# Scores of a windowed attention in 64x64 tiles of the array, with loads and the last steps in another order

## The reference

```python
q, k, v = heads of x @ Wq.T, x @ Wk.T, x @ Wv.T      # 16 heads of 16 features
q, k = l2norm(q), l2norm(k)
rel = pos[None, :] - pos[:, None]                    # key minus query
mask = (rel < 0) | (rel >= 128)                      # a key lies 0 to 127 ahead
attn = softmax(q @ k.T - abs(rel) * slope_of_head, masked)
x = layernorm(x + (attn @ v) @ Wo.T)
w1b, w2b = alpha1 * sign(w1), alpha2 * sign(w2)      # alpha: mean of |w| in a row
x = layernorm(x + gelu(x @ w1b.T + b1) @ w2b.T + b2) # 1024 hidden
```

## Time and profile before

| what | value |
|---|---|
| time, median of 3 runs | 373.69 us (373.42 to 374.68) |
| the profiled execution's own time | 373.84 us |
| its span, first to last instruction | 372.1 us |
| mean granted TensorE clock | 0.992 |
| busy: PE, PEld, DVE, ACT, POOL | 358.0, 243.9, 318.2, 310.0, 274.5 us |
| DMA moved | 38.31 MB |

### The profile page before, as it was taken

The page is one execution under the profiler, slowest core; times in us unless marked ns, Lnnn a source line. Parts: engine busy times, 40 slices in busy tenths (PEclk is TensorE's granted clock), DMA queues, the critical chain, the costliest instruction groups (busy, mean ns, idle before and its releaser), DMA issues.

```text
span 372.1 us, 11965 instructions
## 1 busy us (share of the span) xinstructions
PE 358.0 (96%) x3933; PEld 243.9 (66%) x3933; DVE 318.2 (86%) x856; ACT 310.0 (83%) x539; POOL 274.5 (74%) x418
## 2 busy tenths in 40 slices
PE   8699999999999999999999999999999999999991
PEld 5445567766766776676676667775666666666671
DVE  3967789998898988888998997869789999999995
ACT  3579789888898898898899999887888888887873
POOL 1169999899999999999999999857554754754321
PEclk9989999999999999999999999999999999999998
DMA  6757944564464446467676754303303404404113
GB/s 225 147 80 173 193 93 117 105 121 87 111 124 101 111 100 127 100 156 162 132 140 143 160 106 82 58 3 60 58 0 58 114 18 98 114 17 97 58 57 113
DMA packets 99490, 38.31 MB, mean 103 GB/s; under 512 B 84736, under 2 KB 98432, under 8 KB 99328
## 3 DMA queue, kind: packets, MB, share of 16 engines
q1 hardware_dynamic: 99456, 37.89, 46.7%
HBM read 12.72 MB, written 4.19 MB: 45 GB/s over the span
## 4 chain that ended last, share of the span: by engine, by line
PE 62%; DVE 24%; issue 5%; DMA 4%; SPq 2%; ACT 1%; DVEq 1%; POOL 0%; POOLq 0%
PE ps L392 14%; PE ps L402 13%; PE ps L435 9%; PE ps L372 8%; PE ps L411 6%; DVE prob L1150 4%; DVE w L1150 4%; PE ps L532 4%; PE ps L419 3%; DVE zstats L1170 3%; DVE resid L1198 3%; PE ps L566 2%; PE ps L426 2%; DVE z L1160 2%; SPq L273 2%
## 5 line engine op out<-in xcount | busy, mean ns | idle before, releaser
L1363 POOL TENSOR_SCALAR_AFFINE_SELECT prob<-prob 128x512 f32<-128x512 f32 x252 | 154.4, 648 | 14.0 <-ACT prob L673 13.4
L673 ACT ACTIVATE prob<-ps 128x1024 f32<-128x1024 f32 (+1 forms) x128 | 122.2, 1009 | 11.6 <-PE ps L372 11.5
L402 PE MATMUL ps<-wqkv,xt 128*128 128x512 f32 x124 | 60.4, 610 | 1.4 <-DVE qkn L934 1.1
L532 PE MATMUL ps<-yT,sgn 128*128 128x512 f16 x256 | 61.1, 379 | 0.0
L745 ACT ACTIVATE ps<-ps,bias,alpha 128x512 f32<-128x512 f32 x64 | 47.9, 750 | 15.6 <-PE ps L532 12.5
L1431 POOL TENSOR_TENSOR resid<-z,resid 128x256 f32 (+1 forms) x31 | 22.6, 728 | 46.0 <-DVE z L1160 46.0
L392 PE MATMUL ps<-prob,vdiag 128*17 128x128 f32 x1024 | 51.4, 274 | 0.0
L392 PE MATMUL ps<-prob,vnext 128*17 128x128 f32 x992 | 50.0, 273 | 0.0
L372 PE MATMUL ps<-qkT 64*128 64x256 f16 (+1 forms) x512 | 38.8, 270 | 2.1 <-DMA qkT<-parts 2.1
L532 PEld LDWEIGHTS ps<-yT,sgn 128*128 128x128 f16 x256 | 25.0, 98 | 22.6
L435 PE MATMUL ps<-wo,oT 128*128 128x256 f32 x128 | 36.2, 405 | 0.0
(11 more groups left out here) (115 smaller groups left out, 679.8 us busy)
## 6 DMA issues: line engine op xcount, KB each, us to landing
xt<-in_xT SPq DMA_DIRECT2D x32, 128.0 KB, 2.1
resid<-in_x SPq DMA_DIRECT2D x32, 128.0 KB, 2.2
out_dram<-resid SPq DMA_DIRECT2D x7, 512.0 KB, 2.9
w<-in_w2T SPq DMA_DIRECT2D x1, 1024.0 KB, 8.1
w<-in_w1T SPq DMA_DIRECT2D x4, 256.0 KB, 3.3
w_nat<-in_w SPq DMA_DIRECT2D x4, 256.0 KB, 3.6
wqkv<-in_wqkvT SPq DMA_DIRECT2D x3, 256.0 KB, 4.1
qkT<-parts SPq DMA_TRANSPOSE x32, 4.3
```

The source lines that it names most:

```text
L402: mm = nc.tensor.matmul(ps[:, QK[slot % 2], :], xt[:, slot, k, :], wqkv[:, k, 0:2 * D], start=(k == 0), stop=(k == DC - 1))
L532: mm = nc.tensor.matmul(ps[:, bank, :], sgn1[:, c, P * k:P * k + P], yT[:, par, a, c, :, :], start=(m == 0), stop=(m == 2 * DC - 1))
L673: nc.scalar.activation(to, scored, ACT.Exp, scale=QK_SCALE ** -2).then_inc(exp_done, 1)
L1363: return nc.gpsimd.affine_select(out=at, in_=at, compare_op=ALU.is_ge, fill=0.0, base=-near, pattern=[[0, CH], [1 if near else -1, P]], ch ...
```

## The change

- **Scores.** Each chunk's four matmuls (64 rows of two heads by 128 keys, 256 queries each) become eight: 64 rows by 64 keys, so four tiles of the array, and 192 queries each. The first 64 keys meet the past queries and the first half of the own ones, the last 64 the second half of the past ones and the own ones. The quarter of the window that is left out is masked anyway; the exponential still reads it, so the four banks are cleared once at the start. The order of the products stays: t, then hp, then the key halves.
- **qkT.** Queries must now lie side by side, past then own, so `qkT` is laid out with the slot inside, and has a fifth slot for the queries of slot 0 again. From block 4 on, SP issues a second transpose, of the queries alone, right behind that of slot 0 (7 more in all, half a block each). PE (chunk 0) and ACT (`high_halves`) wait for it at slot 0, on a new semaphore `again_in`.
- **PE waits.** Each chunk also waits for `consts`.
- **Probabilities.** `OWN_AT` and `NEAR_AT` put the near halves at 0 and 1, the own ones at 2 to 5.
- **Loads.** The residual rows of blocks 0 and 1 are issued ahead of block 4's transpose, those of 2 and 3 behind it, with a semaphore each; DVE waits for the first pair in `add_output(0)`, for the second after its step 4.
- **Start.** The first `keep_warm` writes bank 2, the second comes after two waits; DVE clears four more banks.
- **Drain.** `hidden_low(0, 0, 0)` goes ahead of `round_of(NB - 2)`, `row_stats(NB - 4)` behind `hidden_low(0, 1, 0)`.

```diff
-QSLOT = (0, 2, 1, 3)
-OWN_AT, NEAR_AT = (0, 4, 1, 5), (2, 3)
+OWN_AT, NEAR_AT = (2, 3, 4, 5), (0, 1)
...
-        qkT = sb("qkT", [P, XS, 2 * (H // 2), P], F16)
+        qkT = sb("qkT", [P, 2 * (H // 2), XS + 1, P], F16)
...
-                sp.dma_start_transpose(qkT[:, QSLOT[s]],
+                sp.dma_start_transpose(qkT[:, :, s, :],
                                        parts[:, s % 2].rearrange("p h a d -> p (h a d)")).then_inc(qk_in[s % 2], 16)
+                if s == 0 and not (isinstance(n, int) and n == 0):
+                    sp.dma_start_transpose(qkT[:, 0:H // 2, XS, :],
+                                           parts[:, 0, 0:H].rearrange("p h a d -> p (h a d)")).then_inc(again_in, 16)
...
             load_block(XS + 3, 3)
+            for n in range(2):
+                sp.dma_start(resid[:, n, :], x[n]).then_inc(first_resid[0], 16)
             turn_parts(XS, 0)
-            for n in range(XS):
-                sp.dma_start(resid[:, n, :], x[n]).then_inc(first_resid, 16)
+            for n in range(2, XS):
+                sp.dma_start(resid[:, n, :], x[n]).then_inc(first_resid[1], 16)
             load_block(2 * XS, 0)
...
+                pe.wait_ge(consts, 2)
                 if c == 0:
-                    pe.wait_ge(qk_in[par], 8 * (i - par) + 16)
-                count(pe, exp_done, i * NC + c - 1)
-                here, past = QSLOT[slot], QSLOT[(slot - 1) % XS]
-                first, last = (past, here) if par else (here, past)
-                wide = 2 * P if both else P
+                    pe.wait_ge(qk_in[par], turned)
+                    if slot == 0:
+                        count(pe, again_in, again)
+                count(pe, exp_done, taken)
+                queries_at = (slot - 1) * P if slot else (XS - 1) * P
+                windows = ((0, P + P // 2), (P // 2, 2 * P)) if both else ((P, P + P // 2), (P, 2 * P))
                 for t in range(2):
+                    rows_of_queries = qkT[:, 2 * c + t].rearrange("p s q -> p (s q)")
                     for hp in range(2):
                         row = slice(64 * hp, 64 * hp + 64)
-                        queries = qkT[row, first:last + 1:last - first, 2 * c + t, :] if both else qkT[row, here, 2 * c + t, :]
-                        mm = nc.tensor.matmul(ps[:, SC + 2 * (c % 2) + hp, 2 * P * t:2 * P * t + wide],
-                                              qkT[row, here, H // 2 + 2 * c + t, :], queries,
-                                              start=True, stop=True)
+                        for half, (first, last) in enumerate(windows):
+                            keys = slice(P // 2 * half, P // 2 * half + P // 2)
+                            at = queries_at if both else -P
+                            mm = nc.tensor.matmul(ps[keys, SC + 2 * (c % 2) + hp, 2 * P * t + first:2 * P * t + last],
+                                                  qkT[row, H // 2 + 2 * c + t, slot, keys],
+                                                  rows_of_queries[row, at + first:at + last],
+                                                  start=True, stop=True)
                 mm.then_inc(s_done, 1)
...
-            keep_warm(WARM)
+            keep_warm(WARM, QK[1])
...
-            keep_warm(WARM_AGAIN)
             pe.wait_ge(id_made, 2)
             pe.wait_ge(consts, 2)
+            keep_warm(WARM_AGAIN, SC)
...
                 count(act, qk_in[par], 8 * (n - 2 - par) + 16 if not isinstance(n, int) or n >= 2 else 0)
+                if again:
+                    count(act, again_in, (n - 2) * (16 // XS))
...
             def add_output(q):
+                if isinstance(q, int) and q == 0:
+                    dve.wait_ge(first_resid[0], 16 * 2)
...
             nc.vector.memset(ps[:, OT, :], 0.0).then_inc(consts, 1)
+            nc.vector.memset(ps[:, SC:SC + 4, :], 0.0)
...
-            dve.wait_ge(first_resid, 16 * XS)
             step(4, 0, prev_ln=False)
+            dve.wait_ge(first_resid[1], 16 * 2)
...
             second_scale()
+            hidden_low(0, 0, 0)
             round_of(NB - 2, False, True)
             y_row(NB - 6, False)
             row_stats(NB - 5, mv_late[:, 0, :])
-            row_stats(NB - 4, mv_late[:, 1, :])
-            hidden_low(0, 0, 0)
             outputs(NB - 2)
             add_output(NB - 3)
             hidden_low(0, 1, 0)
+            row_stats(NB - 4, mv_late[:, 1, :])
             row_stats(NB - 3, mv_late[:, 2, :])
```

More of the change, by code:

```diff
@@ L210, in build @@
         wv_in, wo_in = sem("wv_in"), sem("wo_in")
-        first_resid = sem("first_resid")
+        first_resid = [sem("first_resid_pair"), sem("second_resid_pair")]
         w2_in, w1t_in, bias_in = sem("w2_in"), sem("w1t_in"), sem("bias_in")
@@ L223, in build @@
         qk_in = [sem("qk_in_even"), sem("qk_in_odd")]
+        again_in = sem("again_in")
         v_done, v_ready = sem("v_done"), sem("v_ready")
@@ L360, in scores @@
             def scores(i, c, par, slot, both):
-                if c == 0:
-                    pe.wait_ge(qk_in[par], 8 * (i - par) + 16)
-                count(pe, exp_done, i * NC + c - 1)
-                here, past = QSLOT[slot], QSLOT[(slot - 1) % XS]
-                first, last = (past, here) if par else (here, past)
-                wide = 2 * P if both else P
+                turned, again, taken = 8 * (i - par) + 16, i * (16 // XS), i * NC + c - 1
+                if not isinstance(i, int):
+                    if c == 0:
+                        turned = pe.to_reg(turned)
+                        again = pe.to_reg(again) if slot == 0 else 0
+                    taken = pe.to_reg(taken)
+                pe.wait_ge(consts, 2)
+                if c == 0:
+                    pe.wait_ge(qk_in[par], turned)
[4 more added lines that the diff above has]
+                windows = ((0, P + P // 2), (P // 2, 2 * P)) if both else ((P, P + P // 2), (P, 2 * P))
                 for t in range(2):
+                    rows_of_queries = qkT[:, 2 * c + t].rearrange("p s q -> p (s q)")
                     for hp in range(2):
                         row = slice(64 * hp, 64 * hp + 64)
-                        queries = qkT[row, first:last + 1:last - first, 2 * c + t, :] if both else qkT[row, here, 2 * c + t, :]
-                        mm = nc.tensor.matmul(ps[:, SC + 2 * (c % 2) + hp, 2 * P * t:2 * P * t + wide],
-                                              qkT[row, here, H // 2 + 2 * c + t, :], queries,
-                                              start=True, stop=True)
+                        for half, (first, last) in enumerate(windows):
[5 more added lines that the diff above has]
+                                                  start=True, stop=True)
                 mm.then_inc(s_done, 1)
@@ L468, in step, with keep_warm @@
                         weighted_sum(i - 2, c, (slot - 2) % XS)
-            def keep_warm(times, bank=SC):
+            def keep_warm(times, bank):
                 for n in range(times):
@@ L630, in root, with high_halves @@
                 nc.scalar.activation(y, ln_, ACT.Exp, scale=-0.5).then_inc(done, 1)
-            def high_halves(n, par, first=False):
+            def high_halves(n, par, first=False, again=False):
                 act.wait_ge(qkn_done, n + 1)
                 count(act, qk_in[par], 8 * (n - 2 - par) + 16 if not isinstance(n, int) or n >= 2 else 0)
+                if again:
+                    count(act, again_in, (n - 2) * (16 // XS))
                 src = qkn[:, par, :].rearrange("p (h d) -> p h d", d=HD)
@@ L659, in step @@
                 own, near = OWN_AT[slot], NEAR_AT[par]
-                at = slice(near, own + 1, own - near) if par else slice(own, near + 1, near - own)
+                at = slice(near, own + 1, own - near)
                 def exps(c):
@@ L671, in exps @@
                         to = prob[:, own, CH * c:CH * c + CH, :]
-                        scored = banks.rearrange("p b (t q) -> p (b t) q", t=2)[:, :, 0:P]
+                        scored = banks.rearrange("p b (t q) -> p (b t) q", t=2)[:, :, P:2 * P]
                     nc.scalar.activation(to, scored, ACT.Exp, scale=QK_SCALE ** -2).then_inc(exp_done, 1)
@@ L677, in step @@
                 if high_first:
-                    high_halves(i + 2, par)
+                    high_halves(i + 2, par, again=slot == 0)
                 exps(0)
```

## The result

The changed kernel takes 370.77 us (median of 5 runs, 370.30 to 371.21) where the kernel before took 373.42 on the same chip. The ratio is 0.9924, with a 95% interval of 0.9901 to 0.9946: faster by 0.76%, or 2.8 us, with 2.0 to 3.7 us for the interval. The forecast was 369.3, which is 4.4 us under the 373.69 that it started from. The profiled execution took 370.34 us, its span is 368.5. One execution of a variant further down, "DVE's additions first", took 513.84 us at a mean granted clock of 0.656, and its median leaves that one out.

The account below looks back on a forecast made before the run. The prediction took TensorE (PE) to bound attention and DVE the hidden layer. Tiles -4.5 us, transpose and residual rows +0.25, drain -0.2 summed to -4.45, giving 369.3 us, range 366.5 to 373.3.

Parts of the forecast that it names:

- Scores in tiles: Attention's score clusters take 0.446 us for 0.54, saving 0.094 each; -4.5 us over all counted steps.
- C: Scores: a group's four loads run one after another and set the pace; +0.04 us a cluster, 375.6 us; chance 0.12.
- D: Scores: column halves don't stream together when row halves do; +0.23 us a cluster, 387 us; chance 0.06.
- Other engines: Attention: 0.16 us to spare before the next cluster's second chunk waits for exponentials, about 0.1 after; ACT doesn't bind.
- Rival F: Attention: ACT or POOL takes over once PE is shorter, at about 7.16 us a block; 371.4 us; chance 0.12.
- Steps 24 to 31: End of attention: steps 29 and 30 gain 0.38 us, step 31 0.1, POOL-held steps 25 to 28 0.1, step 24 fully.
- The extra transpose: SP's queue at slot 0: later ones hidden with 1.9 us to spare; block 4's 1.0 us late, bounds 0 and 2.
- ACT's new wait: ACT at slot 0, for the second transpose: costs nothing, since scores two steps earlier already waited for that landing.
- First residual rows: Steps 4 and 5: sending rows 0 and 1 ahead of the transpose gives back up to 0.75 us.
- Clearing banks and drain: Start: four banks cleared in 1.9 us at most, hidden; drain: new order gains 0.2 us, bounds 0 and 0.5.

Follow-up runs that it names:

- DVE's additions first: The changed kernel with add_output ahead of outputs on DVE in every step, PE's order kept: 371.05 us, 0.9927 of the kernel before.
- narrower windows: The changed kernel with each score tile taking 128 queries for 192 in blocks with both halves: 369.85 us, 0.9923 of the kernel before.
- the shortened last exponential: The changed kernel with chunk 3's exponential taking only the own half in blocks 4 to 23: 368.83 us, 0.9868 of the kernel before.
- the shortened first one: The changed kernel with chunk 0's exponential taking only the own half in blocks 4 to 23: 369.62 us, 0.9893 of the kernel before.
- Old loads: The changed kernel with all four residual rows behind block 4's two transposes, waited for ahead of DVE's step 4: 373.31 us, 1.0006 of the kernel before.

## Why the prediction was right, and where it fell short

The sign, the range and the main mechanism held; the gain was 2.8 us for 4.4. Stage by stage, from the first A of block 0 in each profile, the kernel before run again against the changed one:

| stage | before, us | after, us | difference | forecast |
|---|---|---|---|---|
| first A to A of block 8 | 53.62 | 53.26 | -0.36 | -0.5 |
| A of block 8 to A of block 24 | 116.13 | 114.89 | -1.24 | -3.0 |
| A of block 24 to B of block 31 | 53.03 | 52.89 | -0.14 | -0.8 |
| B of block 31 to the end | 130.56 | 130.35 | -0.21 | -0.2 |

That is -1.95. The first A itself came at 17.14 us for 18.11. Of these 0.97 some 0.45 belong to the change: PE waits 1.87 us for the first transposed block in both profiles of the kernel before, and 1.39 to 1.44 in all twelve with the new `qkT`, whose first transpose lands 4.4 us after its issue for 4.8. That makes 2.4 us. The rest is when that transpose went out, 12.5 to 13.5 us in kernels that are alike up to there. The forecast had no term for the start. Nor had it one for the clock: 23 of 73 executions of the kernel before had a mean granted clock of 0.990 or less, and were 0.5 to 0.8 us longer than those at 0.995 and more; of the changed kernel and its variants with moved loads, 1 of 79 had. By these numbers that is some 0.2 us of the gain, an estimate; which edit does it is not shown.

**Scores in tiles: right.** Forecast were starts 0.11, 0.08, 0.08 and 0.17 apart, 0.446 in all; the single starts are 0.107, 0.082, 0.083 and 0.182 apart, 0.454 (at B; at A the last is 0.188 at three slots of four). The assumption on which all rested, that row and column halves stream together, holds, which ends C and D. PE's own part of a block is 2 x 0.089 shorter, for 2 x 0.094. The load takes 105 ns where one of 128 columns took 94, and the first interval, on which the load shows, is 0.025 over the others; it was 0.01.
The Trainium skill, TensorEngine Tiling (Array Packing), section Restrictions, says that column tiling disables Fast Weight Load. The trace agrees in sign: half the columns take 105 ns for 94, and the first interval is 0.025 us over the others for 0.01.

**Other engines: the step that failed.** The text says "ACT nearly touches, but doesn't bind", and takes every cluster of steps 4 to 24 as 0.094 saved. It checked one wait, that of chunk 1 for the exponentials, and read 0.16 us to spare. Of these, 0.11 are the way from the end of an exponential to the load that it lets go: with narrower windows, where that load does wait, it starts 0.114 after. So 0.05 were to spare, and none are in the changed kernel, where the load starts 0.114 after as well. That costs next to nothing, 0.006 us at A.

What cost was the other way from the exponentials back to PE, through Ln, Exp and DVE to `turn_rows` and `project_v`, which the text did not follow. It had 0.15 us to spare at slots 1 and 2. PE's earlier arrival (0.09) and the Exp, later after A by 0.07, take that; a busy time that leaves 0.5 us "until another engine is reached" doesn't show it. The loss itself, 0.15 and 0.19 us, comes with DVE's first operation, which there runs into POOL's clears. Narrower windows show that PE isn't the bound, the shortened last exponential gives back 0.085 of the 0.093 lost between A and B (4.848 - 4.755), and the shortened first one removes slot 1's loss where that operation is short again. No run moves POOL's clears alone, and DVE's two operations behind the first also take 0.19 or 0.5 us by the block, which I did not follow. In numbers: slots 1 and 2 make 1.35 us in these 16 blocks, slot 0's 0.05 makes 0.2, the clusters' 0.089 for 0.094 makes 0.16, together 1.7 of the 1.8 us by which this stage was forecast too high.

**Rival F** gave 7.16 us a block and 371.4: the period was 7.18, the time 370.8. Its size came true, by luck: its reason, that ACT or POOL has too much work, did not. DVE and ACT are busy 6.4 and 6.2 us of 7.18, POOL 6.86; what took over is a chain of waits through ACT and DVE, and when in it POOL's clears fall.

**Steps 24 to 31: too high a forecast.** I had counted 0.1 for the four blocks that POOL holds, and full gains for steps 24, 29 and 30; 0.14 came in all. Steps 24 and 25 gain in full, A to B 4.76 each, so the loss of the loop isn't there. But in steps 26 to 28 A to B takes 5.38, 4.76 and 5.20 us for 4.84, 5.19 and 4.84: 0.47 longer in all, where I had counted a little gain. Steps 29 and 30 gained 0.07 of the 0.38 counted for them. No run takes these apart. The stage took 52.73 to 52.89 us in the changed kernel and two variants that are alike there, so a gain of 0.14 isn't told from one of 0.3.

**The extra transpose: the later six right, block 4's wrong.** "I take 1.0 late" was wrong. The half transpose went out at 37.01, took 1.33 on the queue and landed 3.2 to 3.8 us after its issue, as all seven did; A of block 4 started at 40.55, 3.54 after it, right behind the weighted sums, with only its 0.21 of issue before it. I had put 2.65 us behind the queue's time, out of the longest landing of a whole block; the half's is 2.2 (3.54 - 1.33) or less. And it went out 2.67 us after the block's first transpose, where I had counted 3.25. It is hidden, with some 0.2 to spare: the shortest of the three landings from 33 to 45 us, this one's, is 3.3. "ACT's new wait" cost nothing that shows, but PE's comes with 0.05 us at every slot 0, for which the sum had no term. The times of the seven, from issue to landing:

```profile
L274 SPq DMA_TRANSPOSE qkT<-parts x7: 1317/1682/1975, 37.0 to 210.3; - x7
DMA to landing us min/median/max: 3.2/3.6/3.8
```

and SP's queue with block 4's scores:

```profile
34.34 2.63 SPq L271 DMA_TRANSPOSE qkT<-parts  x1
...
37.01 1.33 SPq L274 DMA_TRANSPOSE qkT<-parts  x1
38.39 1.06 SPq L297 DMA_DIRECT2D resid<-in_x  x2
...
40.55 0.52 PE L388 MATMUL ps<-qkT 64*64 64x192 f16 x16
```

**First residual rows: the price was of a loss that comes anyway.** DVE's wait is gone. But from A of block 4 to A of block 8 next to nothing is gained: 29.88 us, against 29.79 in the first profile of the kernel before and 29.94 in the second (from the first matmuls). The 0.75 that I read as lost in steps 4 and 5 was 0.0 in the second profile, though DVE waited 0.41 for the rows there; instead steps 6 and 7 took 0.91 too much, A to B 5.19 and 5.41 us. In the changed kernel they take 5.33 and 5.47. POOL is busy 20 of 20 us from 40 to 60 us in both these profiles. So neither the 0.75 of this term nor the 0.75 that the four steps were to gain by the tiles came in, and the 1.0 of the late transpose didn't either: -0.36 for -0.5 in this stage is luck. Old loads show the other side: without the move, step 4 with the extra transpose took 3.9 us more, so the two edits belong together, and I had priced them one by one.

**Clearing banks and drain: right.** The term of 0.2 for the drain can't be told from nothing. PE's wait of 0.57 us at outputs(30) is gone and a new one at outputs(31) came, as said; it is 0.49, so PE's wait was moved more than removed:

```profile
254.18 0.44 PE L443 MATMUL ps<-id,otok 128*128 128x128 f32 x2 [0.49 <-DVE otok L886]
```

## What to carry to other kernels

Before counting a saving once per loop pass, follow every wait of the shortened engine back to its own last work, not only the nearest one. For each, set the time at which the value is ready against the time at which its reader would come to it without the wait: the difference is what there is to spare, however idle the engines look. An operation on that way that takes 0.2 us in one block and 0.5 in the next is a place to look for what another engine does at that moment. Give each of the two ways round (here A to B and B to A) its own term, since one may keep its saving while the other loses it. A transfer put into a queue is priced by what stands behind it, so read an added transfer and a moved one as one edit.

## What the runs showed of the hardware

- Four 64x64 fp16 tiles, two row halves by two column halves, run together: a group of 192 columns goes by every 0.082 us, three quarters of the 0.109 that a pair took for 256.
- A load of 64 columns by 64 rows takes 105 ns, longer than one of 128 by 64, 94 ns.
- A DMA transpose of half a block (128 by 1024 fp16) takes 1.7 us on the queue and 3.6 to land, at the median; a whole one 1.9 and 4.3, and 4.3 in the old layout too. Half the bytes take 0.84 of the time to landing. The first one of an execution landed after 4.8 us in both profiles of the old layout and after 4.3 or 4.4 in the twelve of the new.
- The DVE operation `nt_a` on 33 columns, both inputs in SBUF, took 0.19 to 0.22 us, or longer when it started under one of POOL's clears of `prob`. In blocks 8 to 23 of all fourteen profiles it took 0.25 to 0.67 us 109 times of 224, and each time it ended 0.043 to 0.049 us after the end of that clear.
- A half-clock stretch of 3.4 us (1.2 GHz) at 18 us was in one profile of the kernel before and not in the other, though PE had waited 1.87 us ahead of it in both; the kernel with old loads had one, of 3.4 us, from 47.2 us on, at the end of a wait of PE of 2.2 us in step 4.
